# A recommender kernel on one core: label rows in chunks of ten in a ring of six slots, in place of five in thirteen

## The reference, cut to what matters

```
q1, q2 = attention pooling of x by (w1, b1, w2) and by (w3, b3, w4)
h      = concat(q1, q2) @ w5 + b5                  # 1024 x 300
f6     = h @ w6 + b6
cross  = h[:, iu] * h[:, ju] * (v @ v.T)[iu, ju]   # all 44850 pairs iu < ju
f7     = cross @ w7 + b7                           # w7 is 44850 x 300
out8   = concat(f6, f7) @ w8 + b8                  # 1024 x 300
return einsum('bu,bku->bk', out8, label_embedding) # 1024 x 200
```

## Time and profile before

| | |
|---|---|
| time, median of 3 runs | 1992.28 us (1981.65 to 1993.16) |
| the profiled execution's own time | 1983.79 us |
| its span in the profile | 1982.0 us |
| TensorE busy in the span | 1685.8 us (85%) |
| VectorE | 1458.6 us (74%) |
| ScalarE | 881.6 us (44%) |
| moved by DMA | 590.73 MB, 298 GB/s over the span |
| mean granted TensorE clock | 0.917 |

### The profile page before, as it was taken

How to read it: one execution, slowest core, us unless ns; L and a number is a source line. 1 busy time by engine, 2 the same in 40 slices (tenths; PEclk the granted TensorE clock), 3 DMA queues, 4 the chain that set the end, 5 groups by cost and what they waited for, 6 DMA issues and landing times.

```text
span 1982.0 us, 25089 instructions
## 1 busy us (share of the span) xinstructions
PE 1685.8 (85%) x7476; PEld 1230.0 (62%) x7476; DVE 1458.6 (74%) x5702; ACT 881.6 (44%) x2513; POOL 41.4 (2%) x86
## 2 busy tenths in 40 slices
PE   1446999999999999999999999999899999996000
PEld 0324677777777677777776777777677777773000
DVE  8755998889972257778753677787447777875998
ACT  5335776676854344444433444444244443541000
POOL 0001000100100100000000000000000000000000
PEclk9667999998999999999998999999999999998555
DMA  6426666565744789999996799999868999996993
GB/s 262 174 90 246 228 232 255 211 269 236 285 181 156 272 341 358 358 372 372 409 330 224 284 363 365 359 391 408 271 243 328 359 363 356 420 387 219 395 393 157
DMA packets 112005, 590.73 MB, mean 298 GB/s; under 512 B 13940, under 2 KB 29069, under 8 KB 81661
## 3 DMA queue, kind: packets, MB, share of 16 engines
q1 hardware_dynamic: 81373, 368.22, 49.8%
q10 hardware_dynamic: 27680, 217.89, 28.4%
q0 software_dynamic: 2816, 3.01, 0.4%
HBM read 585.28 MB, written 3.79 MB: 297 GB/s over the span
## 4 chain that ended last, share of the span: by engine, by line
PE 78%; DVE 14%; DMA 4%; issue 2%; ACT 1%; SPq 1%; POOL 0%; ACTq 0%; DVEq 0%; POOLq 0%
PE bank L525 68%; DVE stream L845 8%; PE bank L496 5%; DVE junk L753 4%; DMA sring<-hrows 3%; PE bank L481 2%; PE bank L507 1%; DVE cring L825 1%; PE bank L538 1%; DMA wring<-in_w7p 1%; PE bank L469 1%; ACT absjunk L603 0%; POOL hrows L442 0%; SPq L369 0%; DMA hrows<-hT 0%
## 5 line engine op out<-in xcount | busy, mean ns | idle before, releaser
L525 PE MATMUL bank<-wring,cring 128*128 128x300 f32 x5616 | 1459.2, 422 | 34.0 <-DVE cring L825 26.8
L525 PEld LDWEIGHTS bank<-wring,cring 128*128 128x128 f32 x5616 | 1078.6, 193 | 403.1 <-DVE cring L825 33.4
L669 ACT ACTIVATE wring<-wring,gcol 128x300 f32<-128x300 f32 x1404 | 635.8, 532 | 779.6 <-DMA wring<-in_w7p 419.1
L845 DVE SCALAR_TENSOR_TENSOR stream<-stream,out 128x300 f32<-128x300 f32 x1600 | 644.2, 465 | 3.9 <-ACT out L590 3.9
L825 DVE TENSOR_TENSOR cring<-lefts,sring 128x1024 f32<-128x1024 f32 (+2 forms) x232 | 274.7, 1187 | 177.6 <-PE bank L525 165.1
L753 DVE SCALAR_TENSOR_TENSOR junk<-stream,ubc 128x300 bf16<-128x300 f32 x896 | 357.1, 466 | 0.0
L825 DVE TENSOR_TENSOR cring<-hT,sring 128x1024 f32<-128x1024 f32 (+1 forms) x120 | 144.5, 1206 | 175.4 <-PE bank L525 141.6
L603 ACT ACTIVATE absjunk<-stream 128x300 bf16<-128x300 f32 x448 | 195.7, 439 | 3.4 <-issue 2.2
L845 DVE DVE_READ_ACCUMULATOR stream<-stream,out 128x1 f32 x1600 | 130.8, 82 | 0.0
L481 PE MATMUL bank<-stream,wts 128*32 128x300 f32 x896 | 66.9, 454 | 63.2 <-DVE small L795 63.2
L496 PE MATMUL bank<-poolT,w5sb 128*128 128x64 f32 (+3 forms) x576 | 95.9, 306 | 3.1 <-ACT poolT L590 3.1
(11 more groups left out here) (51 smaller groups left out, 225.1 us busy)
## 6 DMA issues: line engine op xcount, KB each, us to landing
stream<-in_label SPq DMA_DIRECT2D x320, 750.0 KB, 6.9
wring<-in_w7p ACTq DMA_DIRECT2D x164, 1200.0 KB, 8.5
stream<-in_x SPq DMA_DIRECT2D x64, 1050.0 KB, 9.2
sring<-hrows SPq DMA_DIRECT2D x76, 512.0 KB
wring<-in_w7p ACTq DMA_DIRECT2D x8, 1050.0 KB, 6.7
wring<-in_w7p ACTq DMA_DIRECT2D x8, 600.0 KB, 6.8
sring<-hrows SPq DMA_DIRECT2D x16, 176.0 KB
lefts<-hrows SPq DMA_DIRECT2D x20, 128.0 KB, 5.8
```

The lines of the kernel that those rows point to most:

```text
L525: mm = pe.matmul(acc[(g * GB + b) % 4][:, 0:E], lhs, w, start=(t == 0), stop=(t == NT - 1))
L669: ins = nc.scalar.activation(w, w, ACT.Copy, scale=gcol[:, t:t + 1])
L845: ins = nc.vector.scalar_tensor_tensor(out=row_in, in0=row_in, scalar=1.0, in1=out8[:, m % (2 * GB), :], op0=ALU.mult, op1=ALU.mult, accum ...
```

## The change

Two constants are changed. The label rows come in chunks of ten, 1.5 MB or 12000 contiguous bytes for each partition, in six slots. The loads of labels fall from 320 to 160 and the ring from 65 rows to 60. A chunk is now issued on every second step of the phases 1 to 3 (each even u from 12 to 90), on each of the tail's steps, which fall from 80 to 40, and the fill of the ring is six loads in place of thirteen. The tile stream becomes 63 rows in place of 65 (the x ring is the larger now). No arithmetic, no order of rows and no other queue's program is changed.

```diff
@@ -134,9 +134,9 @@
     HALVES = [GS] + [NS - GS] + [0] * (G - 1)
     FIRST = [sum(HALVES[:k]) for k in range(len(HALVES))]
     ROUNDS = [1 << k for k in range(FOLD.bit_length() - 1)]
-    LR = 5
+    LR = 10
     LC = K // LR
-    LSLOTS = 13
+    LSLOTS = 6
     SSLOTS = 2
     CSLOTS = 4
     WSLOTS = 3
```

## The result

The changed kernel takes 2003.7 us in the median (six runs, 1999.53 to 2007.92) against 1993.12 us before (six runs, 1981.65 to 1995.07): a ratio of 1.0061, 95% interval 1.0035 to 1.0086. It is slower by six tenths of a per cent, 10.6 us between the medians and 12 us by the ratio. That is within the 1% that the prediction called no change, and 2003.7 us is inside its range of 1978 to 2006.

The account below looks back on a forecast made before the run. TensorE was taken to bound the long part and VectorE the tail, with label loads hidden. Terms +3.8 (fill), 0 and -2 (phase ends) sum to +1.8 us; on the median 1992.28 that gives 1994.1 us, range 1978 to 2006.

Parts of the forecast that it names:

- the likeliest case: Whole kernel: measured time within 1% of the time before, chance 0.87.
- the rival of whole blocks: Engines take a label load's 8 or 16 packets before w7's: 3.8 us per w7 load, +10.4 us, 2003; chance 0.12.
- the prediction's own signs of being wrong: TensorE gaps inside the 290 us run, VectorE waiting for a label slot in the tail, or another granted clock.
- The fill: Ring fill at phase 1: w7 packets take turns with longer label packets; +3.8 us once, bounds 0 and 7.6.
- The landing of w7: From 860 to 1000 us: w7 loads land 1.9 us later, median 10.6 us; by whole blocks 12.5.
- w7 loads in phases 1 to 3: term 0: Phases 1 to 3: later w7 loads still fit their 14.4 us of room; cost 0, from above 5.7 us.
- The phase ends: Phase 1 to 2 and 2 to 3: step 89's chunk no longer precedes the next unit 0's load; -2 us.
- No cost in the tail: Tail: loads landing in 8 to 12 us stay within 19.6 us of ring reserve; VectorE does not wait, 0.
- Faster loads: Chunks of 1.5 MB move faster, so TensorE's DMA waits shrink: -8 us, 1984 on the median; chance 0.17.
- DMA as the bound: Steady part of phases 1 to 3: slower 12000-byte packets make w7 late at every unit; +26 us, 2020; chance 0.08.

Follow-up runs that it names:

- padded: The changed kernel (ten rows) with the tile stream padded to 65 rows, so every tile lies where it lay before; ratio 1.0042 to the kernel before, stretch 1153.73 us.
- the fill spread: The changed kernel with one label chunk loaded at phase 1's start and the other five at steps 4 to 12; ratio 1.0004 to the kernel before.
- the chunks held back: Kernel before, five-row chunks: fill spread over steps 5 to 10, chunks of steps 82 to 90 in phases 1 and 2 held to the next phase; ratio 0.9864.
- chunks behind w7: The changed kernel with steady-part chunks of phases 1 to 3 waiting for one more TensorE unit, so issued 4.0 us behind w7; ratio 1.0034 to the kernel before.

## Why the prediction was right, and where it was off

The range and the likeliest case (no change by 1%) held; the sum was too small: +1.8 us on the stretch where 10.5 were measured, and 12 by the timed ratio. That the time still lies in the range is owed to the range's width of 28 us, made to take in the dearer rivals, and not to the sum. The measured 2003.7 us is all but the 2003 of the rival of whole blocks, by chance: its turns are not what the runs show. And one of the prediction's own signs of being wrong came true, since TensorE has a gap at 940.88 us inside what had been the run of 290 us.

**The fill** was called +3.8 us by turns, packet by packet. It measured +4.58 and +3.40 (padded), and -0.09 with two DMAs of the same rows. The place and the mechanism are right. The earlier trace rows did not show it, though: 0.70 and 0.59 MB are about one to one by bytes as well as by number; the packets' order shows it, above. That the size came so near is in part luck. The two w7 loads landed 1.1 and 2.9 us later (9.3 and 14.6 us, before 8.2 and 11.7) where 1.9 and 3.8 had been worked out, and the 1.7 us of the lower clock behind the wait were in no term.

**The landing of w7** was called 10.6 us in the median, and by whole blocks 12.5. It measured 10.4 and 9.4, and 10.3 with the fill spread. The number is that of the forecast, but in the steady part most of a chunk goes ahead of the w7 load and only its last packet or two take turns, so the agreement is no proof of the turns; blocks of 16 fit neither the number nor the order of the packets. The Trainium skill's rule ("DMA: Bandwidth & Descriptors", section "Queues, rings and completion order") that an engine drains a group of some 9 to 17 descriptors before it changes is not seen here: at the fill one label packet, or two, stands between two w7 packets. A chunk of ten rows is 8 packets of 12000 bytes on each engine, or 16 of 6000 when two DMAs load it; drained as one block it would keep a w7 load waiting equally long. In the phases, where one chunk comes in 8 us, the two differ: landing 10.4 us against 9.0, mid-phase waits 4.2 us against none.

**"w7 loads in phases 1 to 3: term 0"** is the step that failed. The room of 14.4 us was worked out as four units of 4.04 us from two rows of the steady part, though the units 58 and 59 have four tiles between them and not eight. There the room is three units, 12.1 us, less 1.85 of scaling, 10.3 us; the load issued at 927.64 landed 11.2 us later, and the wait was 1.15 us, about the difference. The price was 4.2 us in three phases. It lay in the table of units, not in a rare row: the size of a unit had to be asked for at each place, not once.

**The phase ends** were called -2 us for the chunks of odd steps that go. TensorE's idle time ahead of the next first unit fell from 2.97 to 2.41 us and from 3.12 to 2.37, in sum by 1.3 us, so the step's place was right. In phase 1 the way from unit 87's product to the next first unit fell from 40.06 us to 38.72, about the 1 us that was put on it. But what is left of each phase after the mid-phase wait is -0.4, +1.2 and +0.9 us, in sum +1.7: the gain at one load was given back at the next (unit 89 waited for 3.79 us, before 1.05). Five rows in twelve slots and in two DMAs have +1.9 and +1.7 for the whole stretch without a longer packet, so 2 us here are within what the trace of one execution scatters, and the term is not told from 0.

**No cost in the tail** was right: 166.05 us against 166.07, so the ring of 60 rows was enough. Label loads landed after 7.9 us, the low end of 8 to 12.

**The rivals.** Faster loads did not come; the Trainium skill's rule on batching to 1 MiB ("DMA: Bandwidth & Descriptors", section "Bandwidth") gave nothing, since the time of a load was hidden in both kernels. DMA as the bound did not come: the share fell from 0.98 to 0.96. What was missed altogether is that the waits at the phase ends, 9.1 us for products and 6.1 put down to issue, were worth more than their rows say, because the granted clock is lower around them too: with the chunks held back two phases are 17 us shorter, some 10 by the waits and up to 7 by the clock.

## What to carry to other kernels

Where two queues share the DMA engines, the size of a packet in one bears on the latency of the other, even where the engines' busy share does not rise (0.98 and 0.96 here); split a bulk load that has time into smaller packets, or keep it away from the moments when the other has no room. Work out the room of a prefetch at its shortest unit of work, and not in the steady state. And a bulk stream with a deep ring can be held back where small serial loads are on the path: here that, with the fill spread, was worth 1.4%, with no instruction saved. Count a wait of TensorE of some 3 us together with the stretch at the lower clock that came behind it here.

## What was not expected of the hardware

- Packet size, at equal bytes and equal times of issue: w7 landing 10.4 us in the median and 13.7 at most beside 12000-byte label packets (9.4 and 13.8 padded), 9.0 and 10.4 beside 6000. With other times of issue: 8.3 beside 2400, and 8.4 with 12000 when the chunk comes 4 us behind.
- The granted clock falls to 0.50 behind waits of TensorE as short as 2.4 us (3.4 us from 700.9 us on in the changed kernel), and the matmuls behind them take longer.
- The phases -1 and 0, the same instructions in all versions but those with an x ring of eight, end between 666.48 us (five rows, twelve slots) and 682.95 us (chunks behind w7). It goes with the granted clock: from 180 us to the first mark it is at the lower level for 34.0 us in the first of the two runs below and for 57.8 us in the second. These stretches are of the run with 666.48 and of the changed kernel with 677.61; the third number from the end is the clock:

```profile
200.00:400.00 200.00, 197.05 (x1119) 140.95 (x1118) 193.09 (x830) 144.32 (x512) 9.02 (x18) 0.97 0.63 237
400.00:650.00 250.00, 250.00 (x1388) 184.11 (x1386) 178.06 (x727) 157.77 (x535) 9.02 (x18) 0.97 0.59 223
```
```profile
200.00:400.00 200.00, 197.05 (x1070) 140.66 (x1072) 188.53 (x811) 140.60 (x499) 9.02 (x18) 0.94 0.62 234
400.00:650.00 250.00, 250.00 (x1396) 182.81 (x1385) 181.74 (x745) 157.78 (x541) 9.02 (x18) 0.95 0.58 220
```

  A clock of 0.03 less over 200 us and of 0.02 less over 250 us is 11 us, the measured difference. Why it was granted less is not known; it is as large as the whole effect of the change, and only marks inside the trace keep the two apart.
